# Six channel-mixing runs inside the last three bodies of a merged transformer and recurrence kernel, and the gated output on GpSimd

## The reference

```
xa = ln(x);  sx = xa shifted by one position - xa
xm[j] = xa + sx * (maa_stack[j] + tanh((xa + sx*maa_x) @ maa_w1)[j] @ maa_w2[j])     # five mixes
w = exp(-exp(time_decay + tanh(xw @ td_w1) @ td_w2));  r, k, v, g = xr@Wr.T, xk@Wk.T, xv@Wv.T, silu(xg@Wg.T)
per step: a = k v^T;  out = r (u*a + s);  s = a + w*s
x1 = x + (groupnorm(out) * gn_w + gn_b) * g @ Wo.T
xc = ln(x1);  sx2 = xc shifted by one position - xc
kk = relu((xc + sx2*ffn_maa_k) @ Wfk.T)^2;  rr = sigmoid((xc + sx2*ffn_maa_r) @ Wfr.T)
return x1 + rr * (kk @ Wfv.T)
```

## Time and profile before

| | |
|---|---|
| median of 3 runs | 1224.46 us (1221.35 to 1226.11) |
| time of the profiled execution | 1226.68 us |
| its span, first to last instruction | 1224.9 us |
| instructions | 35607 |
| merged loop, body 13 begins | 1009.52 us |
| last L1647 of body 15 | 1114.20 us |

### The profile page before, as it was taken

One profiled execution on the slowest core, in us unless ns is written; L12 is line 12 of the kernel. 1 busy time (PEld: TensorE's weight loads), 2 busy tenths in 40 slices (PEclk: granted clock), 3 DMA queues, 4 the chain that ended last, 5 costly groups with the idle time before them and its releaser, 6 DMA issues.

```text
span 1224.9 us, 35607 instructions
## 1 busy us (share of the span) xinstructions
PE 1146.1 (94%) x13568; PEld 969.5 (79%) x13568; DVE 962.9 (79%) x1670; ACT 777.4 (63%) x1750; POOL 591.7 (48%) x520
## 2 busy tenths in 40 slices
PE   5999999999999998999999999999999998777898
PEld 5888898889898876787788877888778886555687
DVE  5987778787777832388999999999999999897554
ACT  5777887777877745654576555765556653455664
POOL 5778777878778720343434434344342443331121
PEclk9999999999999988999999999999999997788999
DMA  8300000111111000000000000000000000000011
GB/s 334 125 4 1 0 1 4 29 46 42 40 43 43 27 2 1 1 1 1 2 1 1 1 2 0 0 0 0 0 0 0 0 2 1 1 1 1 36 52 52
DMA packets 25534, 27.29 MB, mean 22 GB/s; under 512 B 2336, under 2 KB 20064, under 8 KB 25056
## 3 DMA queue, kind: packets, MB, share of 16 engines
q1 hardware_dynamic: 25440, 25.99, 6.3%
HBM read 21.79 MB, written 4.19 MB: 21 GB/s over the span
## 4 chain that ended last, share of the span: by engine, by line
PE 72%; DVE 14%; issue 11%; POOL 2%; ACT 1%; DMA 0%; DVEq 0%; ACTq 0%; POOLq 0%
PE psum L934 9%; PE psum L353 9%; PE psum L943 7%; PE psum L267 5%; PE psum L336 4%; PE psum L368 4%; PE psum L1023 4%; PE psum L1060 4%; PE psum L297 3%; PE psum L280 3%; DVE shared L1653 3%; DVE shared L1647 2%; PE psum L310 2%; PE psum L1104 2%; PE psum L983 2%
## 5 line engine op out<-in xcount | busy, mean ns | idle before, releaser
L1653 DVE TENSOR_TENSOR_SCAN shared<-late_wT,shared 128x512 f32<-128x512 f32 x128 | 184.8, 1444 | 4.4
L849 POOL TENSOR_TENSOR late_xm<-late_mixed,late_xa 128x512 f32<-128x512 f32 x80 | 93.7, 1180 | 160.4 <-DVE late_mixed L1621 154.1
L232 POOL TENSOR_TENSOR shared<-shared,att_row_max 128x512 f32<-128x512 f32 x128 | 132.6, 1055 | 17.0 <-DVE att_row_max L564 17.0
L858 POOL TENSOR_TENSOR shared<-shared,late_rT 128x512 f32<-128x512 f32 x32 | 40.8, 1274 | 185.9 <-DVE shared L1653 185.9
L353 PE MATMUL psum<-shared 128*128 128x128 f32 x1024 | 127.3, 278 | 0.0
L1647 DVE TENSOR_TENSOR shared<-psum,shared 128x504 f32<-128x504 f32 x128 | 86.8, 678 | 47.7 <-PE psum L1060 46.4
L453 ACT ACTIVATE shared<-shared 128x512 f32<-128x512 f32 x128 | 80.4, 631 | 68.9 <-POOL shared L232 68.7
L943 PE MATMUL psum<-w,late_hT 128*128 128x256 f32 x512 | 122.1, 383 | 1.0 <-ACT late_hT L1296 0.9
L934 PE MATMUL psum<-late_glnT,w 128*128 128x256 f32 x512 | 120.3, 389 | 1.8 <-ACT late_glnT L1287 1.8
L353 PEld LDWEIGHTS psum<-shared 128*128 128x128 f32 x1024 | 121.6, 195 | 0.3 <-ACT shared L462 0.2
L564 DVE TENSOR_REDUCE att_row_max<-shared 128x8 f32<-128x512 f32 x128 | 86.8, 680 | 41.0 <-POOL shared L225 41.0
(11 more groups left out here) (160 smaller groups left out, 2675.3 us busy)
## 6 DMA issues: line engine op xcount, KB each, us to landing
shared<-in_enc SPq DMA_DIRECT2D x64, 128.0 KB, 2.6
out<-x SPq DMA_DIRECT2D x16, 256.0 KB, 2.0
x<-in_x SPq DMA_DIRECT2D x7, 512.0 KB, 9.6
w<-in_w SPq DMA_DIRECT2D x2, 1024.0 KB, 17.4
shared<-in_cross_mask SPq DMA_DIRECT2D x1, 1024.0 KB, 11.6
shared<-in_w_qkv SPq DMA_DIRECT2D x1, 768.0 KB, 4.5
x<-in_x SPq DMA_DIRECT2D x2, 256.0 KB, 3.7
shared<-in_w_kv SPq DMA_DIRECT2D x1, 512.0 KB, 12.6
```

Of the source, the lines that this page charges most:

```text
L232: nc.gpsimd.tensor_tensor(zs, zs, peak.unsqueeze(2).to_broadcast([P, PAIRS, S]), ALU.subtract).then_inc(shifted, 1)
L849: nc.gpsimd.tensor_tensor(xm[:, m % 2, :, :].rearrange("p h (b t) -> p (h b) t", t=S), mixed[:, m % 2, :, :].rearrange("p h (b t) -> p (h ...
L1653: nc.vector.tensor_tensor_scan(states, wT[:, u, half, :, :, :].rearrange("p j b t -> p (j b t)"), states, 0.0, ALU.mult, ALU.add).then_inc ...
```

## The change

`EARLY = 6` replaces `TAIL = 4`. Runs 0 to 5 of channel mixing go into bodies 13, 14 and 15, two in each (`early`, `early_run`), where the MLP's instructions stood in earlier bodies. These six use the MLP's PSUM bank for all four stages (`ch_bank`), so each product waits until the one before it in that bank has been read. The run with even number is finished within the body, the odd one at the start of the next. Runs 6 to 9 take the places that runs 0 to 3 had after the bodies, and runs 10 to 15 follow, written out without a loop. The channel norm has three parts: runs 0 to 9 (variances in body 12), 10 to 12 (body 15) and 13 to 15. `ch_kk` and `ch_rr` lie in the place of the MLP's weight w1 instead of that of the repeated values. In every body the product of the normed output with the gate moves from VectorE to GpSimd, behind `make_bonus` and ahead of `step_back`; its factor 0.5 goes into the norm's scale and bias (`half_gn`).

```diff
-TAIL = 4
+EARLY = 6
...
-        ch_kk, ch_rr = (spare[:, i * 2 * HALVES * RT:(i + 1) * 2 * HALVES * RT].rearrange("p (u n) -> p u n", u=2)
+        ch_kk, ch_rr = (core.weights["w1"][:, i * 2 * HALVES * RT:(i + 1) * 2 * HALVES * RT].rearrange("p (u n) -> p u n", u=2)
                         for i in range(2))
-        ch_tr, ch_key, ch_recept, ch_value = mlp, proj, v_banks[0], v_banks[1]
+
+        def ch_bank(stage, r):
+            if stage == "tr":
+                return proj if r == EARLY else mlp
+            return mlp if r < EARLY else {"key": proj, "recept": v_banks[0], "value": v_banks[1]}[stage]
+
 
         names = ("gxn_ready gxnT_ready gln_ready up_ready gelu_ready down_ready mlp_bias mlp_x run_stats_ready moments_ready "
...
-        NORMS = ((0, (RUNS - 3) * CH), ((RUNS - 3) * CH, RUNS * CH))
+        NORMS = ((0, (RUNS - 6) * CH), ((RUNS - 6) * CH, (RUNS - 3) * CH), ((RUNS - 3) * CH, RUNS * CH))
...
+
         def channel_runs(eng, body):
-            for s in range(TAIL, TAIL + 2):
-                body(s, s % 2)
-            with eng.Fori(TAIL // 2 + 1, RUNS // 2 - 2) as i:
...
 
+            def apply_gate(r, u):
+                pool.wait_ge(gate_done, r + 1)
+                pool.wait_ge(onT_copied, r + 1)
+                if later(r):
+                    pool.wait_ge(out_ready, r)
+                nc.gpsimd.tensor_tensor(yT[:, :], onT[:, :], gates[:, u, :], ALU.mult).then_inc(y_ready, 1)
...
+                if there(s - 2):
+                    apply_gate(s - 2, u)
                 if there(s + 1):
                     step_back(s + 1)
...
+                    if n == 2 and early(s):
+                        ch_shift(early_run(s, 0), 0)
...
+                    if n == 3 and early(s):
+                        ch_shift(early_run(s, 1), 1)
...
-            channel(0, 0)
+            apply_gate(RUNS - 2, 0)
+            ch_shift(EARLY + 1, 1)
+            channel(EARLY, 0)
             scale(RUNS - 1)
-            channel(1, 1)
-            channel(2, 0)
-            channel(3, 1)
+            channel(EARLY + 1, 1)
+            apply_gate(RUNS - 1, 1)
+            channel(EARLY + 2, 0)
+            channel(EARLY + 3, 1)
...
                         if now:
                             project(s, NG)
+                        if early(s - 1):
+                            ch_values(early_run(s - 1, 1), 1)
...
                             project_out(s - 2)
                         if mlp_run:
                             mlp_transpose(s + 3)
+                        if early(s):
+                            ch_transpose(early_run(s, 0), 0)
                         if mixing:
...
                             mix_pair(s + 1, 0)
+                        if early(s):
+                            ch_transpose(early_run(s, 1), 1)
...
+                        if early(s):
+                            ch_keys(early_run(s, 0), 0)
...
                         sum_heads(s, 0)
                         sum_heads(s, 1)
+                    if n == 4 and early(s):
+                        ch_receptances(early_run(s, 0), 0)
...
                         mix_last(s + 1)
+                    if n == 5 and early(s):
+                        ch_values(early_run(s, 0), 0)
                     if n == 6:
                         if mixing:
                             decay(s + 1)
                             project(s + 1, NK)
+                        if early(s):
+                            ch_keys(early_run(s, 1), 1)
+                        if s_is(s, RUNS - 1):
+                            ch_transpose(EARLY, 0)
...
                         project(s + 1, NR)
+                    if n == 7 and early(s):
+                        ch_receptances(early_run(s, 1), 1)
...
                     if n == 7 and norm:
                         transpose(s + 2)
-                    if s_is(s, RUNS - 1):
-                        if n == 4:
-                            ch_transpose(0, 0)
-                        if n == 5:
-                            ch_transpose(1, 1)
-                        if n == 7:
-                            transpose_on(RUNS - 2)
-                            ch_keys(0, 0)
-                            ch_receptances(0, 0)
+                    if n == 7 and s_is(s, RUNS - 1):
+                        transpose_on(RUNS - 2)
 
             def ch_transpose(r, u):
                 pe.wait_ge(ch_xn_ready, r + 1)
-                if not later(r):
+                if r == 0:
                     pe.wait_ge(mlp_x, RUNS)
+                elif r == EARLY:
+                    pe.wait_ge(gate_done, RUNS)
+                elif r < EARLY and r % 2 == 0:
+                    pe.wait_ge(ch_rv_ready, r)
+                elif r == EARLY + 1:
+                    pe.wait_ge(ch_rv_ready, EARLY)
                 else:
                     pe.wait_ge(ch_xc_ready, r)
...
-                    pe.wait_ge(gate_done, RUNS)
+                if r < EARLY and r % 2 == 0:
+                    pe.wait_ge(ch_xc_ready, r + 2)
+                elif r < EARLY:
+                    pe.wait_ge(ch_rv_ready, r)
+                elif r == EARLY:
+                    pe.wait_ge(ch_xc_ready, EARLY + 1)
                 else:
                     pe.wait_ge(ch_relu_ready, r)
...
-                if not later(r):
+                if r < EARLY:
+                    pe.wait_ge(ch_relu_ready, r + 1)
+                elif r == EARLY:
...
-                if not later(r):
+                if r < EARLY:
+                    pe.wait_ge(ch_rr_ready, r + 1)
+                elif r == EARLY:
...
+            ch_values(EARLY - 1, 1)
             project_out(RUNS - 2)
+            ch_keys(EARLY, 0)
             sum_heads(RUNS - 1, 2)
             sum_heads(RUNS - 1, 3)
-            ch_transpose(2, 0)
+            ch_transpose(EARLY + 1, 1)
             transpose_o(RUNS - 1)
-            ch_keys(1, 1)
-            ch_values(0, 0)
-            ch_receptances(1, 1)
-            channel(1, 1)
+            ch_receptances(EARLY, 0)
+            channel(EARLY, 0)
             transpose_on(RUNS - 1)
-            channel(2, 0)
+            channel(EARLY + 1, 1)
             project_out(RUNS - 1)
-            channel(3, 1)
+            channel(EARLY + 2, 0)
+            channel(EARLY + 3, 1)
             channel_runs(pe, channel)
...
-                                                ACT.Identity, scale=col(core, "gn_w", half), bias=col(core, "gn_b", half))
+                                                ACT.Identity, scale=half_gn[:, 0, half:half + 1], bias=half_gn[:, 1, half:half + 1])
...
-            def ch_nonlinear(r, u):
+            def ch_square(r, u):
                 act.wait_ge(ch_key_ready, r + 1)
...
-                    act.wait_ge(vj_ready, RUNS * GROUPS_R)
-                nc.scalar.activation(ch_relu[:, :], ch_key, ACT.Relu).then_inc(ch_relu_ready, 1)
+                nc.scalar.activation(ch_relu[:, :], ch_bank("key", r), ACT.Relu).then_inc(ch_relu_ready, 1)
                 act.wait_ge(ch_relu_ready, r + 1)
+                if r == 0:
+                    act.wait_ge(up_ready, RUNS * UPS)
                 if later(r - 1):
                     act.wait_ge(ch_value_ready, r - 1)
                 nc.scalar.activation(ch_kk[:, u, :], ch_relu[:, :], ACT.Square).then_inc(ch_kk_ready, 1)
+
+            def ch_tanh(r, u):
...
-                nc.scalar.activation(ch_rr[:, u, :], ch_recept, ACT.Tanh, scale=0.5).then_inc(ch_rr_ready, 1)
...
+            def ch_nonlinear(r, u):
+                ch_square(r, u)
+                ch_tanh(r, u)
...
                     copy(s, u, NG)
+                if early(s):
+                    ch_normalise(early_run(s, 0), 0)
+                    ch_normalise(early_run(s, 1), 1)
                 if there(s):
                     repeat_values(s, u, 2)
                     repeat_values(s, u, 3)
+                if early(s):
+                    ch_copy_in(early_run(s, 0), 0)
                 if there(s + 3):
...
-                if s_is(s, RUNS - 1):
-                    ch_normalise(0, 0)
-                    ch_normalise(1, 1)
-                    ch_copy_in(0, 0)
-                    ch_normalise(2, 0)
+                if early(s):
+                    ch_copy_in(early_run(s, 1), 1)
+                    if s_is(s, RUNS - 1):
+                        ch_normalise(EARLY, 0)
+                    ch_square(early_run(s, 0), 0)
                 if there(s + 1):
                     copy(s + 1, 1 - u, NW)
+                if early(s):
+                    ch_tanh(early_run(s, 0), 0)
                 if there(s - 1):
                     square(s - 1)
...
                     make_decays(s + 1, 1 - u)
+                if early(s):
+                    ch_square(early_run(s, 1), 1)
+                if there(s + 1):
                     repeat_values(s + 1, 1 - u, 1)
...
-                if s_is(s, RUNS - 2):
+                if s_is(s, RUNS - 4):
                     ch_invert(0)
+                if s_is(s, RUNS - 1):
```

(74 more changed lines are left out.)

38 lines of the change are left out of this document (19 added, 19 removed).

## The result

The changed kernel takes 1234.92 us (median; 1231.42 to 1239.39), the kernel before beside it 1223.75: ratio 1.0094, 95% interval 1.0074 to 1.0114. It is slower by some 11 us, where no measurable change was forecast, and it lies above the range. The profiled execution took 1234.04 us with a span of 1232.3. Lines have moved: the recurrence's product L1647 is now L1723, `spread` L1060 is L1081, `mix_pair` L983 is L1004, `project_out` L1104 is L1125, `transpose_on` is L1116, `ch_transpose` L1218, `ch_keys` L1234, `ch_receptances` L1248, `ch_values` L1263, `ch_mix` L1824, `ch_finish` L1832 and L1836, and the gate, on GpSimd, L872.

What follows compares the result with a forecast made beforehand. TensorE was taken to bound the steady bodies and the end, VectorE bodies 13 to 15. The terms -33.6 + 9.0 + 7.9 + 8.1 + 8.4 - 1 = -1.2 gave 1223 us on the median, range 1208 to 1234.

Steps and rivals of the forecast that it cites:

- the ends of bodies 13 and 14: From VectorE's last mix to the next body: 8.2 us for 3.7 (+4.5) in 13, 7.1 for 3.7 (+3.4) in 14.
- rival (c): TensorE's half clock spreads through the body ends and after them: +12.7 on -1.2, about 1236 us; chance 0.18.
- the 1.4 counted in body 15: Half of the 2.7 us that half clock would add to body 15's keys, transposes and group 7.
- the six freed runs: Six channel runs leave the last stage at full pace, 5.60 us each: -33.6 us.
- keys(1): At body 13's end, the odd run's keys wait for the first half of `ch_finish(0)` to free the PSUM bank.
- keys(7): After the bodies, these keys come at +17.6 us, where keys(1) came at 10.72 before: +6.9.
- the slow `mix_pair`: Body 13, before group 3: TensorE idles 3.2 us, its clock falls, the pair takes 2.08 us again; group 3 is +2.8.
- the gate's move: In the 11 steady bodies, the gate on GpSimd shortens `project_out`'s wait: -1 us, bounds -7 and +3.
- `ch_mix(1)` in group 4: Body 13, VectorE: the odd run's mix has no idle time to cover it and costs +1.7 us.
- the 2.9 at group 2: Start of body 14: the odd run's finish before group 1, a later `step_back` and a waiting `ch_transpose(2)` make +2.9 us.
- One run early: After the bodies, `transpose_on(15)` stands one run earlier in TensorE's queue than ScalarE can serve: 40.1 us for 38.57, +1.5.
- (a): VectorE's work is all that counts: -33.6 + 14.9 = -18.7, about 1206 us, bodies of 42 to 44 us; chance 0.28.

Runs made afterwards that it cites:

- e4b: The changed kernel with useless TensorE products right before each odd early run's keys, so that only the clock changes; 1227.68 us, ratio 1.0037.
- e5: The changed kernel with four early runs instead of six, none in body 13; 1231.01 us, ratio 1.0078.
- e11: e8 with four early runs instead of six; 1215.09 us, ratio 0.9938.
- e10: e8 with the odd early run's mix ahead of the recurrence's mix 2 in VectorE's group 4; 1213.82 us, ratio 0.9913.
- e7: The changed kernel with the last transposes and last output product one channel run later in TensorE's queue; 1226.20 us, ratio 1.0025.
- e8: The changed kernel with the even early run's finish moved to group 5's end and the last transposes and output product later; 1212.85 us, ratio 0.9911.

## Why the prediction was wrong

The mechanism that the prediction named was there, the terms of its sum were not: it priced the ends of bodies 13 and 14 at full clock, the odd run's mix in group 4 at its time alone, and the stretch after the bodies without the wait that stands in it. The first, and the clock's part of the last, belong to what it had set aside as rival (c). I estimate the clock at half of the 12.1 us by which the sum missed: 2.1, 1.3 and 0.3 in the bodies (from e4b, less the 1.4 counted in body 15) and some 2.6 behind the wait of 4.52 us, where eight keys and two sets of transposes took 5.8 us for some 3.1 at full clock.

- **The steps that held.** TensorE at the bound in the steady bodies, VectorE in the last three; the six freed runs; keys(1) waiting on the first half of `ch_finish(0)`; VectorE idle 3.58 and 2.49 us before its last products; keys(7) at 18.0 us for 17.6; the slow `mix_pair` (2.08 us behind 4.00 idle, I had assumed the same 2.08; with what stands behind it group 3 of body 13 starts 3.5 us later for the 2.8 forecast); the gate's move, -1.6 for -1. Bodies 51, 48 and 37.5 us long stood where I had 47, 46 and 37.
- **The ends of bodies 13 and 14: +4.5 and +3.4 were counted at full clock.** The prediction noted an idle of about 4.5 us before the keys and that every idle of 3.2 us and more in the earlier trace rows is followed by half clock, counted half of it in body 15 and none here, and gave (c) a chance of 0.18. The wait was 4.93 us, the keys took 3.75. e4b puts the clock at 2.1, 1.3 and 1.7 us in the three bodies: half of body 13's miss of 4.0, half of body 14's 2.5. As (c) put it (2.6, 6.3 and 1.3 more than my sum, 2.5 after), body 13 was near and body 14 far too high: its 12.7 came out close to the 12.1 measured by luck, with other parts.
- **`ch_mix(1)` in group 4: +1.7.** It costs 3.2: groups 4 to 5 are 9.3 us apart (1037.76 - 1028.45), 6.1 before (1035.46 - 1029.34), through 2.59 us for the products and 1.48 for the reading, beside GpSimd's additions. That is 1.5 more of body 13. The same step is the other half of body 14's miss: its group 4 is 2.2 us longer for the 0.7 counted. Two small parts are left, 0.7 us more at body 13's `mix_pair` and 0.5 less in group 5 of both bodies. e5 and e11 show that body 14 starts slower with early runs ahead of it (first group 7.48 for 5.65, and 7.86 for 5.71); that was in the sum, in the 2.9 at group 2. e10 shows that the overlap cannot simply be ordered away.
- **"One run early": +1.5 after the bodies.** It was 5.8: the stretch gives back 13.1, of which 7.3 lie before keys(7) (18.0 - 10.72). e7, which undoes the early place, takes 6.3 out. I followed ScalarE's and GpSimd's queues to keys(7) by rows, but priced what comes after it by a comparison with the old stretch. The wait to work out was TensorE's own: `square`, a table load, the logarithm, `scale`, 4.52 us in which nothing behind `transpose_on(15)` in TensorE's queue can go, and the clock behind it. Rival (c) names this wait, at about 4.6 us; the sum leaves it out.
- **The range.** 1208 to 1234 was said to take in most of (a) and (c), but their own sums, 1206 and 1236, both lie outside it. With 0.18 given to (c), the upper end stood 2 us under (c)'s own time; the measured 1234.92 fell between.

**The gain.** 33.6 us were freed and came out as a loss of 11. Half of the 44.5 us between the two has one cause: a step placed in an in-order queue behind (or ahead of) what does not need it. Two placements gave 22 us back (e8), and the result then lies between the forecast and (a): body lengths of 44.5 and 44.1 are close to the 42 to 44 of (a). What is left to (a)'s 1206 are the tail's price (6.8 us of the 33.6: 83.85 - 110.66 + 33.6) and 1 us a body more than the 14.9 that (a) counted (44.46, 44.08 and 34.07 us are 17.9 over before).
